# Selecting the top 128 keys of 32 attention heads: the row tiles of a head taken widest first instead of narrowest first

## The chip, the cores and the metric

The kernel runs on one core of a Trainium2 chip. A core has TensorE (PE, matmuls), VectorE (DVE), ScalarE (ACT), GpSimd (POOL) and SyncE (SP), each with an instruction stream of its own; they meet by semaphores. The metric is the time of one execution on the device in microseconds (us), lower is better. The kernel before takes 3154.21 us, the median of three runs (3152.70 to 3154.62).

## The reference, cut to what matters

The reference is a network of two layers on 1024 tokens: MLPs, a Mamba layer, and an attention layer with 32 heads of 16 features. The change is in the attention layer alone. There each row keeps its 128 largest causal scores and takes the softmax over these:

```python
draft = jnp.einsum('bhqd,bhkd->bhqk', qr, kr)
draft = draft + jnp.where(causal_future, neg, 0.0)
num_remain = max(min(Sq, MIN_REMAIN), Sq - int(Sq * MASK_OUT))      # 128 for Sq = 1024
_, draft_indices = jax.lax.top_k(draft, num_remain)
mask = jnp.full((B, H, Sq, Sq), neg).at[b_idx, h_idx, s_idx, draft_indices].set(0.0)
mask = jnp.where(causal_future, neg, mask)
scores = jnp.einsum('bhqd,bhkd->bhqk', qr, kr) / np.sqrt(HD) + mask
attn = jax.nn.softmax(scores, axis=-1)
out = jnp.einsum('bhqk,bhkd->bhqd', attn, v)
```

## The kernel before, in words

The function `attention_heads_fast` does the 32 heads. The 1024 query rows of a head are 8 row tiles of 128 rows; tile t needs only the keys up to its diagonal, (t + 1) * 128 columns. Tiles 1 to 7 (256 to 1024 columns) have more keys than 128 and need a selection; tile 0 has not. `W` is 7, `NT` is 8.

A head passes these steps. They lie in different iterations n of one loop, so that four or five heads are under way at once:

- *Scores and evacuation* (head n+1): PE computes the scores of a tile into `ps_z` (`scores`, L1943), DVE copies them to `z` in SBUF and keeps the row maximum (`evacuate`, L2256).
- *Sweeps* (heads n and n-1): ACT counts, per row, how many scores lie above a trial cut, by a Sign activation with an accumulator (`count`, L2090, the instruction is L2101). One sweep is seven counts, one for each tile. POOL then moves the trial cut (`move`, L2171). A head has four sweeps (k = 0 to 3); in an iteration ACT does (n, 0), (n-1, 2), (n, 1), (n-1, 3). The move behind sweep 3 gives the final cut (L2210), a little under 128 scores.
- *Marks and picks* (head n-2): DVE marks the scores above the cut (`take`, L2269), PE computes the scores again in `ps_m` with the marked ones put out of reach (`marked_scores`, L1959), DVE takes the eight largest that are left and replaces as many of them as are missing to 128 (`pick`, L2287: MAX8 at L2296, MATCH_REPLACE8 at L2304; `excess`, L2278, counts how many).
- *Exponents and values* (head n-3): for each chunk of up to four 128 column blocks of a tile PE turns the picked scores and subtracts the row maximum (`exponents`, L1997), ACT takes the exponential (`exponential`, L2105, the instruction is L2112), PE multiplies by V (`add_v`, L2022, done two chunks later). `CHUNKS` (L1820) numbers the 12 chunks of a head, in the order of the tiles.
- *Division* (head n-4) on DVE.

All orders are written out by hand. On PE the tables `CHUNK_AHEAD`, `CHUNKS_FIRST`, `CHUNKS_AFTER_MARKED` and `CHUNKS_AFTER_SCORES` say behind which tile's marked scores or scores a chunk's exponents stand. On ACT, `EXP_BEFORE` spreads the 12 Exps over the 28 counts of an iteration by the share of columns swept; each slot takes the Exp one chunk back (`LATER`). The buffers that tie the engines together: `ps_m` and `ps_z` have two banks each, which a tile of 640 columns or more fills, so the marked scores of the next wide tile wait for the pick of this one; `ps_e` has two buffers; marks and signs have two buffers. `stay_awake` issues seven filler matmuls a round into `ps_m`. The last heads have tables of their own (`LAST_BUT_ONE`, `LAST_CHUNKS`), and from head 29 on odd tiles put their marked scores in `ps_z`.

Of the kernel before, what the change touches and what calls it, by code (L numbers as in the profile page):

```python
# [1812 lines left out]
def attention_heads_fast(nc, env, X, qT, kT, v, mixed, q_tok, k_sums, ahead):  # L1813
# [27 lines left out]
    with ExitStack() as ctx:  # L1841
# [89 lines left out]
        def _(pe):  # L1931
# [27 lines left out]
            def marked_scores(h, t):  # L1959

                L, out = (t + 1) * P, marked_in(h, t)
                pe.wait_ge(take_done, h * W + t)
                if h < NO_SCORES:
                    done = h * W + t - 1 - (1 < t < 4)
                elif t >= 4:
                    done = h * W + t - 2
# [30 lines left out]
            def exponents(h, i):  # L1997
# [501 lines left out]
```

## Time and profile before

| | |
|---|---|
| median of 3 runs | 3154.21 us |
| profiled execution, its own time | 3158.36 us |
| its span, first to last instruction | 3156.5 us |
[...]
| PE, DVE, ACT, POOL busy over the span | 92%, 78%, 62%, 52% |
| stage of the heads | about 2067 to 3041 us |

The page of the profile covers the whole span, of which the heads are less than a third; the shares of the table are means over stages with different limits. The section of rows below therefore shows stretches of that stage. In a timeline a row is an instruction (or several merged, xN) with its start and duration; in brackets stands the idle time of the engine before it and what ended it. An ACT or DVE instruction's duration overlaps the next one's start by about 0.1 us, so distances between starts are what adds up.

### The profile page before, as it was taken

Reading aid. Unit: us, or ns where it says so; the run is one execution under the profiler, and the core shown is the slowest. Engines: PE = TensorE matmul, PEld = TensorE weight load, DVE = VectorE, ACT = ScalarE, POOL = GpSimd, SP = SyncE. Lnnn points to the kernel's source line nnn. Section 1 sums busy time; section 2 is a strip of 40 time slices with the busy share of each in tenths; the row PEclk is TensorE's granted clock in tenths of the full one; section 3 lists DMA queues with packets and bytes.
Section 4 is the critical chain, followed back from the end, with each engine's and each line's share of the span. In section 5 each row is a group of like instructions: output and inputs, shape, how many; then the busy total and the mean of one; then the engine's idle time right before and its main releaser. Section 6 shows DMA issues by size and latency. Waiting matters only on the chain. (4 is left out here: it accounts for less than half of the span.)

```text
span 3156.5 us, 50555 instructions
## 1 busy us (share of the span) xinstructions
PE 2899.5 (92%) x15929; PEld 1723.7 (55%) x15929; DVE 2461.0 (78%) x4633; ACT 1950.0 (62%) x4186; POOL 1651.6 (52%) x3659
## 2 busy tenths in 40 slices
PE   8899999999999999999999989847888888889889
PEld 4455455455454464454554554515666666667654
DVE  6678687697696796796876877749898899988846
ACT  2464554554564554554545533478999999999823
POOL 3236245254264263362462454767777777777613
PEclk9999999999999999999999999958899999998989
DMA  2223122232232132232221220000000000000000
GB/s 92 65 73 102 67 93 88 72 104 72 74 118 84 61 114 80 67 108 73 81 94 67 90 86 1 28 24 1 2 2 2 2 2 2 2 2 2 2 28 27
DMA packets 65947, 169.62 MB, mean 54 GB/s; under 512 B 11920, under 2 KB 19472, under 8 KB 64656
## 3 DMA queue, kind: packets, MB, share of 16 engines
q1 hardware_dynamic: 54016, 114.12, 11.5%
q10 hardware_dynamic: 11664, 52.24, 4.8%
q8 instruction: 131, 2.15, 0.3%
q14 instruction: 136, 1.11, 0.1%
HBM read 161.08 MB, written 5.24 MB: 53 GB/s over the span
## 5 line engine op out<-in xcount | busy, mean ns | idle before, releaser
L2101 ACT ACTIVATE X<-ah_z,ah_trial 128x256 bf16<-128x256 f32 (+6 forms) x896 | 736.3, 834 | 24.8 <-POOL ah_trial L2205 12.8
L1199 ACT ACTIVATE m_mix<-m_mix,m_cs 128x128 f32<-128x128 f32 x1024 | 312.9, 388 | 258.6 <-DMA m_mix<-cs_rows 258.6
L2031 PE MATMUL ah_ps_o<-a_v,X 128*128 128x17 f32 x2304 | 316.9, 264 | 0.1
L2031 PEld LDWEIGHTS ah_ps_o<-a_v,X 128*128 128x128 f32 x2304 | 300.0, 199 | 1.4 <-issue 0.2
L1081 POOL TENSOR_TENSOR m_xdec<-m_xdt,m_decay_out 128x512 f32<-128x512 f32 x112 | 141.4, 1262 | 213.0 <-DVE m_xdt L1325 202.1
L1109 POOL TENSOR_TENSOR m_squares<-m_squares 128x256 f32<-128x256 f32 x128 | 102.3, 799 | 277.5 <-ACT m_squares L1211 277.5
L2275 DVE TENSOR_SCALAR_CACHE_REDUCE X<-ah_z,ah_cut 128x256 bf16<-128x256 f32 (+6 forms) x224 | 193.8, 876 | 60.6 <-POOL ah_cut L2210 60.6
L1005 PE MATMUL m_ps_d<-m_w_out,m_gate 128*128 128x512 f32 x512 | 235.2, 602 | 0.0
L1005 PE MATMUL m_ps_x<-m_w_out,m_gate 128*128 128x512 f32 x512 | 233.7, 599 | 0.0
L2112 ACT ACTIVATE X<-ah_ps_e 128x512 f32<-128x512 f32 (+3 forms) x384 | 187.8, 490 | 62.7 <-PE ah_ps_e L2018 52.6
L2296 DVE MAX8 ah_top<-ah_ps_m 128x8 f32<-128x384 f32 (+6 forms) x215 | 177.1, 824 | 26.0 <-PE ah_ps_m L1983 25.3
L2266 DVE TENSOR_SCALAR_CACHE_REDUCE ah_z<-ah_ps_z 128x256 f32<-128x256 f32 (+6 forms) x224 | 182.5, 816 | 13.9 <-PE ah_ps_z L1955 13.9
L2197 POOL TENSOR_TENSOR ah_slope<-ah_between,ah_table 128x7 f32<-128x7 f32 x128 | 193.2, 1510 | 0.0
L1332 DVE TENSOR_TENSOR m_mix<-m_mix,m_cb 128x1024 f32<-128x1024 f32 x128 | 172.9, 1351 | 19.4 <-ACT m_mix L1202 19.0
L2101 ACT ACTIVATION_READ_ACCUMULATOR X<-ah_z,ah_trial 128x1 f32 x896 | 185.9, 207 | 0.0
L1979 PE MATMUL ah_ps_m<-a_kT,a_qT 128*128 128x512 bf16 (+3 forms) x337 | 107.0, 356 | 84.9 <-DVE tables L2304 84.9
L1172 ACT ACTIVATE m_xbc<-m_xbc 128x1024 f32<-128x1024 f32 x80 | 84.6, 1058 | 148.0 <-DVE m_xbc L1308 147.8
L2304 DVE MATCH_REPLACE8 tables<-ah_top,ah_ps_m 128x384 bf16<-128x384 f32 (+6 forms) x215 | 173.9, 809 | 0.3 <-issue 0.3
L1066 POOL TENSOR_TENSOR m_xdt<-m_w_proj 128x256 f32<-128x256 f32 x32 | 23.8, 742 | 286.1 <-PE m_ps_d L879 286.1
L1308 DVE SCALAR_TENSOR_TENSOR m_xbc<-m_b_tok,m_conv_p,m_xbc 128x1023 f32<-128x1023 f32 (+2 forms) x96 | 129.7, 1351 | 44.6 <-ACT m_xbc L1164 42.4
L879 PE MATMUL m_ps_y<-hT,m_w_proj 128*128 128x512 f32 x320 | 152.0, 597 | 5.3 <-ACT m_gate L1144 3.3
L973 PE MATMUL m_ps_c<-m_mix,m_xdt 128*64 128x128 f32 x2048 | 141.0, 280 | 16.6 <-DVE m_y L1351 8.4
(328 smaller groups left out, 7565.4 us busy)
## 6 DMA issues: line engine op xcount, KB each, us to landing
m_mix<-cs_rows SPq DMA_DIRECT2D x128, 512.0 KB, 4.4
m_w_proj<-in_w_proj ACTq DMA_DIRECT2D x69, 512.0 KB, 3.3
m_fade<-fade_rows SPq DMA_DIRECT2D x224, 128.0 KB, 3.0
m_w_out<-in_w_out ACTq DMA_DIRECT2D x7, 2048.0 KB, 7.8
X<-in_x SPq DMA_DIRECT2D x8, 256.0 KB, 6.4
m_w_out<-in_w_out SPq DMA_DIRECT2D x1, 2048.0 KB, 10.1
x_away<-X SPq DMA_DIRECT2D x1, 2048.0 KB, 7.3
out<-X SPq DMA_DIRECT2D x8, 256.0 KB, 2.0
```

Of the source, the lines that this page charges most:

```text
L879: last = pe.matmul(out, weights[:, k, :], tokens[:, k, :], start=start and k == 0, stop=stop and k == KH - 1, skip_group_check=True)
L1005: last = pe.matmul(ps_out[c % 2], gate[:, half * 4 + i, c * P:(c + 1) * P], w_out[:, half * 4 + i, :], start=(half == 0 and i == 0), stop= ...
L1199: act.activation(mix[:, u % 3, h, :], mix[:, u % 3, h, :], ACT.Relu, bias=cs[:, c, h0 + h:h0 + h + 1], scale=-1.0).then_inc(lag_done, 1)
L1332: dve.tensor_tensor(mix[:, u % 3], mix[:, u % 3], cb[:, c, :].unsqueeze(1).to_broadcast([P, HU, P]), ALU.mult).then_inc(mix_done, 1)
L2031: last = pe.matmul(ps_o[:, t, :], eT[:, g % 3, b * P:(b + 1) * P], v[:, b0 + b, h // REP, :], start=i == 0 and b == 0, stop=b0 + b == t, s ...
L2101: act.activation(sign[:, at % 2, 0:(t + 1) * P], z[:, h % RING, cols(t)], ACT.Sign, bias=trial[:, h % RING, 0, t - 1:t], scale=-1.0, accum ...
L2112: act.activation(eT[:, g % 3, 0:w * P], ps_e[g % 2][:, 0:w, :].rearrange("p b q -> p (b q)"), ACT.Exp, scale=0.25).then_inc(exp_done, 1)
L2197: pool.tensor_tensor(slope[:, 0], between[:, 1], table[:, 5], ALU.pow).then_inc(own, 1)
L2266: dve.tensor_scalar(z[:, h % RING, cols(t)], ps_z[:, z_at(t):z_at(t) + (t + 1) * P], 0.0, NEG, ALU.add, ALU.max, accum_out=row_max[:, h % ...
L2275: dve.tensor_scalar(mark[:, (h * W + t) % 2, 0:(t + 1) * P], z[:, h % RING, cols(t)], cut[:, h % 2, t - 1:t], 0.0, ALU.is_ge, ALU.add, acc ...
L2296: dve.max(top[:, r], marked_in(h, t)).then_inc(pick_step, 1)
L2304: dve.match_replace(picked[:, h % 2, cols(t)], top[:, r], marked_in(h, t), TAKEN).then_inc(pick_done, 1)
```

## The change

All engines take the tiles 7, 6, ..., 1 of a head instead of 1, 2, ..., 7: in scores and evacuation, sweeps, marks, marked scores and picks. The chunks are numbered from tile 7 down to tile 0, so the exponents, Exps and products with V follow that order too. The tables that place the chunks on PE are written anew, the slots for the Exps follow from the new order of column counts, and the semaphore values are computed by `place` and `z_place`. Tile 0's scores stay first. The rule for sharing `ps_m` and `ps_z` among the last three heads is adapted. No instruction is added or removed on PE, DVE and POOL; ACT's stream is the same but for merging of equal neighbours in listings.

```diff
+    ORDER = range(NT - 1, 0, -1)
-    CHUNKS = [(t, b) for t in range(NT) for b in range(0, t + 1, 4)]
+    CHUNKS = [(t, b) for t in range(NT - 1, -1, -1) for b in range(0, t + 1, 4)]
...
-    CHUNKS_AFTER_MARKED = ((), (), (), (), (), (7,), (9,), ())
-    CHUNKS_AFTER_SCORES = ((), (2,), (3, 4), (5,), (6,), (8,), (10,), (11,))
-    LAST_BUT_ONE = ((), (2, 3), (4, 5, 6), (7, 8, 9, 10, 11), (), (), (), ())
-    LAST_CHUNKS = ((), (), (), (), (0, 1), (2, 3), (4, 5), (6, 7))
+    CHUNKS_AFTER_MARKED = ((), (), (11,), (10,), (8,), (6,), (4,), (2,))
+    CHUNKS_AFTER_SCORES = ((), (), (), (), (9,), (7,), (5,), (3,))
...
+        place = lambda h, t: h * W + W - t
+        z_place = lambda h, t: h * NT + (NT - t) % NT
...
                 L, out = (t + 1) * P, marked_in(h, t)
-                pe.wait_ge(take_done, h * W + t)
+                at = place(h, t)
+                pe.wait_ge(take_done, at + 1)
                 if h < NO_SCORES:
-                    done = h * W + t - 1 - (1 < t < 4)
+                    done = at - (t < 3)
...
-                for t in range(1, NT):
+                for t in ORDER:
                     if live(n - 2):
                         marked_scores(n - 2, t)
                     if live(n - 3):
                         turn_and_add(n - 3, CHUNKS_AFTER_MARKED[t])
                     if live(n + 1):
                         scores(n + 1, t)
-                    if live(n - 2) and t == 4:
+                    if live(n - 2) and t == 5:
                         turned_rows(n - 2)
...
                 for back, k in sweeps_of(n):
-                    for t in range(1, NT):
+                    for t in ORDER:
...
                 if live(n - 2):
-                    take(n - 2, 1)
-                    take(n - 2, 2)
+                    take(n - 2, W)
+                    take(n - 2, W - 1)
                 if live(n - 4):
                     divide(n - 4)
-                for t in range(1, NT):
+                for t in ORDER:
                     if live(n - 2):
                         pick(n - 2, t)
                     if live(n + 1):
                         evacuate(n + 1, t)
-                    if live(n - 2) and t + 2 < NT:
-                        take(n - 2, t + 2)
+                    if live(n - 2) and t > 2:
+                        take(n - 2, t - 2)
```

In PE's instruction stream, behind the last filler matmuls of a round (the L2040 row, L2045 in the changed kernel, whose lines lie three to six further down), stand in the kernel before:

```order
L2040 MATMUL ah_ps_m<-a_kT,ident_bf 128x512 x3
L1977 MATMUL ah_ps_m<-future_bf,ident_bf 128x128
L1979 MATMUL ah_ps_m<-a_kT,a_qT 128x256
L1983 MATMUL ah_ps_m<-X,ah_ident_taken 128x256
L1953 MATMUL ah_ps_z<-future_bf,ident_bf 128x128
L1955 MATMUL ah_ps_z<-a_kT,a_qT 128x256
L2010 MATMUL ah_ps_e<-ah_ident_back,tables 128x128 x3
L2012 MATMUL ah_ps_e<-ah_rows,ah_minus_rows 128x384
L2015 MATMUL ah_ps_e<-a_qT,a_kT 128x128 x3
L2018 MATMUL ah_ps_e<-ident_bf,future_bf 128x128
```

and in the changed kernel:

```order
L2045 MATMUL ah_ps_m<-a_kT,ident_bf 128x512 x3
L1984 MATMUL ah_ps_m<-a_kT,a_qT 128x512
L1982 MATMUL ah_ps_m<-future_bf,ident_bf 128x128
L1984 MATMUL ah_ps_m<-a_kT,a_qT 128x512
L1988 MATMUL ah_ps_m<-X,ah_ident_taken 128x512 x2
L2015 MATMUL ah_ps_e<-ah_ident_back,tables 128x128 x4
L2017 MATMUL ah_ps_e<-ah_rows,ah_minus_rows 128x512
L2020 MATMUL ah_ps_e<-a_qT,a_kT 128x128 x4
L2036 MATMUL ah_ps_o<-a_v,X 128x17 x4
L1958 MATMUL ah_ps_z<-a_kT,a_qT 128x512
```

The first marked scores (`ah_ps_m`, L1977 to L1983) are those of the 1024 column tile instead of the 256 column one. The chunk of exponents (`ah_ps_e`) behind them has four blocks instead of three, and the new scores (`ah_ps_z`) stand behind this chunk.

In ACT's stream, from the first count of an iteration to the first of its second sweep, stand in the kernel before (L2101 is a count, L2112 an Exp):

```order
L2101 ACTIVATE X,ah_signs<-ah_z,ah_trial 128x256
L2112 ACTIVATE X<-ah_ps_e 128x512
L2101 ACTIVATE X,ah_signs<-ah_z,ah_trial 128x384
L2101 ACTIVATE X,ah_signs<-ah_z,ah_trial 128x512
L2101 ACTIVATE X,ah_signs<-ah_z,ah_trial 128x640
L2112 ACTIVATE X<-ah_ps_e 128x128
L2101 ACTIVATE X,ah_signs<-ah_z,ah_trial 128x768
L2112 ACTIVATE X<-ah_ps_e 128x256
L2101 ACTIVATE X,ah_signs<-ah_z,ah_trial 128x896
L2101 ACTIVATE X,ah_signs<-ah_z,ah_trial 128x1024
L2101 ACTIVATE X,ah_signs<-ah_z,ah_trial 128x256
L2112 ACTIVATE X<-ah_ps_e 128x384
```

and in the changed kernel, from the Exp that opens the iteration to the Exp that opens the second sweep:

```order
L2117 ACTIVATE X<-ah_ps_e 128x128
L2106 ACTIVATE X,ah_signs<-ah_z,ah_trial 128x1024
L2106 ACTIVATE X,ah_signs<-ah_z,ah_trial 128x896
L2117 ACTIVATE X<-ah_ps_e 128x512
L2106 ACTIVATE X,ah_signs<-ah_z,ah_trial 128x768
L2106 ACTIVATE X,ah_signs<-ah_z,ah_trial 128x640
L2117 ACTIVATE X<-ah_ps_e 128x512
L2106 ACTIVATE X,ah_signs<-ah_z,ah_trial 128x512
L2106 ACTIVATE X,ah_signs<-ah_z,ah_trial 128x384
L2106 ACTIVATE X,ah_signs<-ah_z,ah_trial 128x256
L2117 ACTIVATE X<-ah_ps_e 128x512
L2106 ACTIVATE X,ah_signs<-ah_z,ah_trial 128x1024
```

The counts fall from 1024 to 256 columns, the Exps of the first sweep are of 128, 512 and 512 columns, and the third chunk's Exp (chunk 2) stands ahead of the second sweep's first count instead of behind it.

In DVE's stream, from the first mark of a round (the L2275 row, L2281 in the changed kernel) to the first replacement, stand in the kernel before:

```order
L2275 TENSOR_SCALAR X,ah_taken_count<-ah_z,ah_cut 128x256
L2275 TENSOR_SCALAR X,ah_taken_count<-ah_z,ah_cut 128x384
L2311 RECIPROCAL ah_inv<-ah_ps_o 128x8
L2313 TENSOR_TENSOR hT<-ah_ps_o,ah_inv 128x8x16
L2284 TENSOR_SCALAR ah_surplus<-ah_ranks,ah_taken_count 128x8
L2296 MAX ah_top<-ah_ps_m 128x8
L2298 COPY_PREDICATED ah_top<-ah_surplus,ah_taken 128x8
L2284 TENSOR_SCALAR ah_surplus<-ah_ranks,ah_taken_count 128x8
L2304 MATCH_REPLACE tables<-ah_top,ah_ps_m 128x256
```

and in the changed kernel:

```order
L2281 TENSOR_SCALAR X,ah_taken_count<-ah_z,ah_cut 128x1024
L2281 TENSOR_SCALAR X,ah_taken_count<-ah_z,ah_cut 128x896
L2317 RECIPROCAL ah_inv<-ah_ps_o 128x8
L2319 TENSOR_TENSOR hT<-ah_ps_o,ah_inv 128x8x16
L2290 TENSOR_SCALAR ah_surplus<-ah_ranks,ah_taken_count 128x8
L2302 MAX ah_top<-ah_ps_m 128x8
L2304 COPY_PREDICATED ah_top<-ah_surplus,ah_taken 128x8
L2290 TENSOR_SCALAR ah_surplus<-ah_ranks,ah_taken_count 128x8
L2310 MATCH_REPLACE tables<-ah_top,ah_ps_m 128x1024
```

The two marks ahead of the first pick are the widest two, and the first pick is that of the widest tile.

## Rows read from the trace of the kernel before

**Rows 1.** Busy time by stretch; a round at half clock below:

```profile
core 0: us, PE busy (x) PEld busy (x) DVE busy (x) ACT busy (x) POOL busy (x), PEclk, DMA share, GB/s
2600.00:2700.00 100.00, 87.33 (x817) 67.46 (x816) 89.91 (x245) 97.53 (x247) 77.90 (x280) 0.97 0.01 2
2647.50:2654.00 6.50, 6.50 (x38) 4.93 (x36) 5.98 (x15) 4.67 (x13) 5.82 (x17) 0.51 0.00 1
```

**Rows 2.** Waits of ACT, 2200 to 2800 us: total, times, longest:

```profile
ACT X L2112 <- PE ah_ps_e L2018: 19.0, 22, 2.3
```

**Rows 3.** Timeline of DVE, first mark of a round: start, duration, names, idle before:

```profile
2181.87 0.48 DVE L2275 TENSOR_SCALAR_CACHE_REDUCE X<-ah_z,ah_cut 128x256 bf16<-128x256 f32 x1 [1.29 <-POOL ah_cut L2210]
...
2610.03 0.48 DVE L2275 TENSOR_SCALAR_CACHE_REDUCE X<-ah_z,ah_cut 128x256 bf16<-128x256 f32 x1 [1.10 <-POOL ah_cut L2210]
...
2637.83 0.48 DVE L2275 TENSOR_SCALAR_CACHE_REDUCE X<-ah_z,ah_cut 128x256 bf16<-128x256 f32 x1 [1.10 <-POOL ah_cut L2210]
...
2667.13 0.48 DVE L2275 TENSOR_SCALAR_CACHE_REDUCE X<-ah_z,ah_cut 128x256 bf16<-128x256 f32 x1 [1.87 <-POOL ah_cut L2210]
...
2951.32 0.48 DVE L2275 TENSOR_SCALAR_CACHE_REDUCE X<-ah_z,ah_cut 128x256 bf16<-128x256 f32 x1 [2.33 <-POOL ah_cut L2210]
```

**Rows 4.** Timeline of ACT, one iteration of 27.81 us:

```profile
2604.86 0.51 ACT L2101 ACTIVATE X<-ah_z,ah_trial 128x256 bf16<-128x256 f32 x1
...
2611.44 0.52 ACT L2101 ACTIVATE X<-ah_z,ah_trial 128x256 bf16<-128x256 f32 x1
...
2623.07 0.38 ACT L2112 ACTIVATE X<-ah_ps_e 128x256 f32<-128x256 f32 x1 [0.33 <-PE ah_ps_e L2018]
...
2632.67 0.51 ACT L2101 ACTIVATE X<-ah_z,ah_trial 128x256 bf16<-128x256 f32 x1
```

**Rows 5.** Timeline of POOL, first and last instructions of moves:

```profile
2618.65 0.21 POOL L2175 TENSOR_TENSOR ah_trial<-ah_signs,ah_table 128x7 f32<-128x7 f32 x1 [1.01 <-ACT X L2101]
...
2632.01 0.21 POOL L2205 TENSOR_TENSOR ah_trial<-ah_trial,ah_slope 128x7 f32<-128x7 f32 x1
2632.92 0.20 POOL L2175 TENSOR_TENSOR ah_trial<-ah_signs,ah_table 128x7 f32<-128x7 f32 x1 [0.70 <-ACT X L2101]
```

**Rows 6.** Timeline of PE, a 512 column matmul at half clock:

```profile
2647.51 0.63 PE L2012 MATMUL ah_ps_e<-ah_rows,ah_minus_rows 128*128 128x512 bf16 x1
```

**Rows 7.** Timeline of PE in an undisturbed round:

```profile
2610.58 0.23 PE L1977 MATMUL ah_ps_m<-future_bf,ident_bf 128*128 128x128 bf16 x1 [0.46 <-DVE X L2275]
...
2618.30 0.38 PE L1979 MATMUL ah_ps_m<-a_kT,a_qT 128*128 128x512 bf16 x1 [1.40 <-DVE tables L2304]
...
2622.81 0.22 PE L2018 MATMUL ah_ps_e<-ident_bf,future_bf 128*128 128x128 bf16 x1
...
2628.01 0.39 PE L2010 MATMUL ah_ps_e<-ah_ident_back,tables 128*128 128x128 bf16 x4
...
2628.67 1.02 PE L2031 MATMUL ah_ps_o<-a_v,X 128*128 128x17 f32 x8
2630.34 0.38 PE L1979 MATMUL ah_ps_m<-a_kT,a_qT 128*128 128x512 bf16 x1 [0.66 <-DVE tables L2304]
...
2631.26 0.39 PE L1955 MATMUL ah_ps_z<-a_kT,a_qT 128*128 128x512 bf16 x1
```

**Rows 8.** Timeline of DVE: a narrow mark's accumulator read, the widest mark:

```profile
2610.43 0.08 DVE L2275 DVE_READ_ACCUMULATOR X<-ah_z,ah_cut 128x1 f32 x1
...
2626.44 1.28 DVE L2275 TENSOR_SCALAR_CACHE_REDUCE X<-ah_z,ah_cut 128x1024 bf16<-128x1024 f32 x1
2627.64 0.08 DVE L2275 DVE_READ_ACCUMULATOR X<-ah_z,ah_cut 128x1 f32 x1
```

**Rows 9.** Instructions by line and shape, 2200 to 2800: busy, mean ns, idle before:

```profile
L2112 ACT ACTIVATE X<-ah_ps_e 128x512 f32<-128x512 f32 x127 | 75.7, 596 | 1.1 <-PE ah_ps_e L2015 1.1
...
L2296 DVE MAX8 ah_top<-ah_ps_m 128x8 f32<-128x1024 f32 x21 | 25.9, 1233 | 6.8 <-PE ah_ps_m L1983 6.8
...
L2304 DVE MATCH_REPLACE8 tables<-ah_top,ah_ps_m 128x1024 bf16<-128x1024 f32 x21 | 25.5, 1215 | 0.0
```

**Rows 10.** Timeline of PE, last products with V of the stage:

```profile
3037.69 3.08 PE L2031 MATMUL ah_ps_o<-a_v,X 128*128 128x17 f32 x22
```

More of the change, by code:

```diff
@@ L1836, in attention_heads_fast @@
     MOVE_AT = {hk: i for i, hk in enumerate(order)}
-    sign_share = np.cumsum([0] + [t + 1 for _ in SWEEPS for t in range(1, NT)])
+    sign_share = np.cumsum([0] + [t + 1 for _ in SWEEPS for t in ORDER])
     sign_share = sign_share / sign_share[-1]
@@ L1945, in scores @@
                 L, at = (t + 1) * P, z_at(t)
-                done = h * NT + t - (0 < t < 4)
-                if done:
+                done = z_place(h, t) - (t < 3)
+                if done > 0:
                     pe.wait_ge(z_done, done)
@@ L1982, in marked_scores @@
                     w = min(BANK, L - n)
-                    last = pe.matmul(out[:, n:n + w], ident_taken[:], mark[:, (h * W + t) % 2, n:n + w], start=False, stop=True,
+                    last = pe.matmul(out[:, n:n + w], ident_taken[:], mark[:, at % 2, n:n + w], start=False, stop=True,
                                      skip_group_check=True)
@@ L2006, in exponents @@
                 if t:
-                    pe.wait_ge(pick_done, h * W + t)
+                    pe.wait_ge(pick_done, place(h, t) + 1)
                     for b in range(w):
@@ L2269, in take @@
             def take(h, t):
-                if t == 1:
+                at = place(h, t)
+                if t == W:
                     dve.wait_ge(cut_done, h + 1)
-                if h * W + t > 2:
-                    dve.wait_ge(marked, h * W + t - 2)
-                dve.tensor_scalar(mark[:, (h * W + t) % 2, 0:(t + 1) * P], z[:, h % RING, cols(t)], cut[:, h % 2, t - 1:t], 0.0,
+                if at >= 2:
+                    dve.wait_ge(marked, at - 1)
+                dve.tensor_scalar(mark[:, at % 2, 0:(t + 1) * P], z[:, h % RING, cols(t)], cut[:, h % 2, t - 1:t], 0.0,
                                   ALU.is_ge, ALU.add, accum_out=taken_count[:, h, t - 1:t]).then_inc(take_done, 1)
             def excess(h, t):
-                at = h * W + t - 1
+                at = place(h, t)
                 if at >= 2:
@@ L2287, in pick @@
             def pick(h, t):
-                at = h * W + t - 1
+                at = place(h, t)
                 r = at % 2
@@ L2334, in _ @@
                 if live(n - 2):
-                    take(n - 2, 1)
-                    take(n - 2, 2)
+                    take(n - 2, W)
+                    take(n - 2, W - 1)
                 if live(n - 4):
                     divide(n - 4)
-                for t in range(1, NT):
+                for t in ORDER:
                     if live(n - 2):
@@ L2343, in _ @@
                         evacuate(n + 1, t)
-                    if live(n - 2) and t + 2 < NT:
-                        take(n - 2, t + 2)
+                    if live(n - 2) and t > 2:
+                        take(n - 2, t - 2)
             h = AH - 1
-            take(h, 1)
-            take(h, 2)
+            take(h, W)
+            take(h, W - 1)
             divide(h - 2)
-            for t in range(1, NT):
+            for t in ORDER:
                 pick(h, t)
-                if t + 2 < NT:
-                    take(h, t + 2)
-                if t == 4:
+                if t > 2:
+                    take(h, t - 2)
+                if t == 5:
                     divide(h - 1)
```

35 lines of the change are left out of this document (19 added, 16 removed).

## The prediction

> **What bounds the kernel now.** I first looked at where the change acts: the stage of the 32 heads, about 2067 to 3041 us. Outside it no instruction moves. The reader's first view is the busy time by stretch [rows 1]: of 100 us ScalarE (ACT) is busy 97.5, VectorE (DVE) 89.9, TensorE (PE) 87.3, GpSimd (POOL) 77.9. So ACT is nearly full, and what it still waits for matters: 19.0 us in 600, all of it for exponents (`ah_ps_e`) from PE [rows 2].
>
> Next I measured the round, which handles one head on every engine. It is the distance between two starts of the first mark on DVE, called T0 here. The 28 starts from 2181.87 to 2951.32 [rows 3] are 27 rounds in 769.45 us, 28.50 each. Of these, 12 last 27.80 to 27.82, as 2610.03 to 2637.83; 15 are longer, as the 29.30 to 2667.13. Against 27 x 27.80 = 750.6 the long ones cost 18.9 together.
>
> Then the timeline of one 27.80 us round tells what closes it. T0 is 2610.03; the Exp of 256 columns (chunk 7, tile 5, blocks 4 and 5) starts at 2623.07, after ACT waited 0.33 for it [rows 4]: 13.04 from T0. ACT's remaining work runs to 2632.67: 9.60. POOL starts the last move at 2632.92 [rows 5]: 0.25. The cut is out and the next T0 comes at 2637.83: 4.91. The sum is 27.80, the whole round. It is a loop, cut, marks and picks on DVE, exponents on PE, Exp and sweeps on ACT, move on POOL, back to the cut. ACT's own work is 2604.86 to 2632.67 less 0.33: 27.48. [...] The page's chain of waits shows nothing of this stage, so the argument goes by the timeline.
>
> **What the change moves.** No instruction is added or taken away, so the busy time of each engine stays. What moves is which chunk of exponents each Exp needs, when PE can have it, and where it stands among ACT's sweeps.
>
> *Chunk 2.* In the new order it is tile 6, blocks 0 to 3, placed on PE behind the marked scores of tile 7 (1024 columns); on ACT its Exp stands at the head of the second sweep. Today chunk 2 stands behind the marked scores of the 256 column tile. From T0 to its Exp, step by step:
> - the 1024 column mark on DVE, 2626.44 to 2627.64: 1.20 [rows 8];
> - from its accumulator read to PE, 2610.43 to 2610.58: 0.15 [rows 7, 8];
> - marked scores of tile 7 on PE, 2630.34 to 2631.26: 0.92 [rows 7];
> - exponents of four blocks, 2628.01 to 2628.67: 0.66 [rows 7];
> - from the last matmul to Exp, 2622.81 to 2623.07 less the matmul's own slot of 0.055 (a quarter of the 0.22 for four, from the same rows): 0.20 [rows 4, 7].
>
> That is 3.13 after T0. With 0.25 + 4.91 from the end of ACT's round to T0 it is 8.29 after ACT began its round. ACT wants it earlier. Its first sweep takes 2604.86 to 2611.44 = 6.58 today, with Exps of 512, 128 and 256 columns among the counts; in the new order they are 128, 512 and 512, so for one 0.60 stands instead of 0.38 [rows 4, 9]: about 6.79. ACT stands at that Exp for 8.29 - 6.79 = 1.50 us and, being in order, holds the sweep behind it. Behind it lie 27.48 - 6.79 = 20.69 of ACT's work. The new loop is 3.13 + 20.69 + 0.25 + 4.91 = 28.98, so 1.18 more than 27.80. Over 27 rounds: **+31.9 us**.
>
> *The other Exps.* The 0.33 that goes is in this sum already. The next tight place is chunk 4, behind the marked scores of tile 6, which wait for tile 7's pick. Two marks (1.20 and a little less), a maximum of 1.23 and a replacement of 1.22 [rows 9], and about 1.1 for the short operations between them put that pick's end near T0 + 5.8. PE adds a hand-over, marked scores and four blocks, near 1.9 in all: T0 + 7.7. ACT comes to that Exp at 3.13 and what stands between, two Exps and the counts of four wide tiles, near 7.8. That is an estimate by the rows above; it costs nothing, and at most 0.3 a round (two hand-overs of 0.15), +8 us.
>
> *POOL.* Between the second sweep's end and the last move it now works 2618.65 to 2632.21 = 13.56, and waits 0.70 [rows 5]. The third and fourth sweeps lose the 0.33 and have one Exp of 256 for one of 512 (-0.21). So 0.16 is left and POOL stays hidden, but only just.
>
> *DVE.* It waits 1.10 for the cut today [rows 3], and more in a longer round. The second mark (896 columns) covers PE's first marked scores, 0.92 [rows 7]. DVE's wait for PE at the last wide tiles goes; it lies behind the Exp that closes the loop, so I give it nothing. The evacuations that now come wide first are read by ACT a round later.
>
> *The clock of PE.* Today a half clock stretch costs a long round 18.9 / 15 = 1.26 on average, since the loop reaches PE only at chunk 7 with slack ahead. PE's long wait now is the 1.40 ahead of tile 4 [rows 7]. In the new order PE is done with its filler matmuls long before the 1024 column mark ends: today it waits 0.46 for a mark of 0.40 (2610.03 to 2610.43) [rows 3, 7, 8]; with the mark 0.80 and the round 1.18 longer that becomes about 2.4, and directly behind this wait stand the matmuls that the loop is made of. At half clock 0.92 + 0.66 = 1.58 is doubled at once, and the chunks behind it, which have 0.1 to 0.8 of slack, slip too. Bounds per fall: 1.58 and about 2.6 (half of the 6.5 us of such a stretch is 3.2, less the waits of 0.6 in it). I take 2.1, nearer the middle because both ends rest on rows, and 12 falls in 27 rounds, a little under today's 15 long ones, since some of those are only 0.3 to 0.5 long: 25 against 18.9, **+6**. With no falls it is -18.9; with one in each round +38.
>
> [...]
>
> *The ends of the stage.* At its start the evacuations pace ACT as before in sum: 0. At its end PE is the bound: its last 22 products run 3.08 from 3037.69 and end the stage [rows 10]. Ten chunks of head 30 and all of head 31 follow the last cut; in the new order chunks 0 and 1, done before it, hold 8 blocks, not 3. Five blocks of 0.66 / 4 and two products each of 0.11 to 0.14 (3.08 / 22) make 2.0 to 2.2, of which I take **-1.9 us**; the bounds are 0, if ACT's Exps pace the end, and -4.
>
> Sum: 31.9 + 6 - 1.9 = +36 on the profiled execution's 3158.4, which is 3194. That execution is 4.2 above the median of the runs, so the forecast is 3154.2 + 36 = 3190.
>
> **Rivals.**
> 1. *Few falls of the clock.* PE's waits are shared out otherwise and PE keeps full clock: 31.9 - 18.9 - 1.9 = +11, so 3165. For it: 12 of 27 rounds already run undisturbed. Against it: the longest wait grows.
> [...]
> 3. *Faster: ACT becomes the sole bound.* The place is the same Exp. If chunk 2 is ready by the 6.8 us at which ACT gets there, nothing holds ACT in any round, DVE's and PE's slack absorbs the clock, and a round is ACT's 27.48: 27 x (28.50 - 27.48) = 27.5 less, with the end 29 less, so 3125. It decides at a hand-over 1.5 us sooner than my sum. For it: most chunks get more time when the wide tiles are picked first. Against it: each of the five terms is a row.
> 4. *No difference*: about half the 1.50 is hidden by something that I take as serial, 27 x 0.5 less, and few falls: near 3154.
>
> **How the numbers follow.** Forecast (3176 to 3208) 0.55, rival 1 0.20, rival 2 0.12, rival 3 0.08, rival 4 0.05. About 0.2% is what a measurement of this kernel can tell from no change (6 us). The lower end of rival 1 gives 0.01 to "same": faster 0.08, same 0.06, slower 0.86. The range 3162 to 3220 holds the forecast, most of rival 1 and the lower part of rival 2, and leaves out rivals 3 and 4.
>
> **What would show it.** Right: a wait of ACT of about 1.5 us at the 512 column Exp that opens the second sweep, in each round, for PE; the 0.33 at the 256 column Exp gone; undisturbed rounds of 29.0; PE waiting about 2.4 for the 1024 column mark; POOL's wait before the last move near 0.16. Wrong: rounds of 27.5 and no such wait; or the wait at another Exp (chunk 4), or POOL without a wait ahead of the last move, which would make it the bound. If long rounds exceed 28.98 by under 1 us or are rare, the clock term is mis-sized and the time is nearer 3165.

## The result, and the profile after

The changed kernel takes 3246.9 us (median of 4 runs, 3232.56 to 3266.45) against 3153.9 for the kernel before: 1.0297 times as long, 95% interval 1.0271 to 1.0324. The forecast was 3190 with a range to 3220. The direction was right, the size was not. The profiled execution took 3232.56, the lowest of the four, with a span of 3230.7; before it was 3156.5 [rows 1 to 10 are from it]. The readings of this section compare these two spans, 74.2 apart. The medians are 93 apart: the profiled execution of before is 4 above its median, that of the changed kernel 14 below. The other three runs of the changed kernel have a lower mean clock (0.938 to 0.945 against 0.948; the profiled execution of before has 0.963), so more of the clock's loss is in them; no trace shows their rounds.

The busy time by stretch, columns as in [rows 1]: the same 100 us as there, then one undisturbed round, one long round, and the 27 us inside it.

```profile
2600.00:2700.00 100.00, 87.14 (x714) 67.39 (x714) 80.84 (x217) 86.45 (x218) 68.71 (x246) 0.85 0.01 2
...
2463.90:2492.78 28.88, 24.22 (x225) 18.84 (x226) 25.68 (x69) 27.12 (x69) 22.00 (x79) 0.94 0.01 2
2615.73:2653.31 37.58, 34.91 (x224) 27.46 (x225) 26.43 (x69) 27.70 (x68) 22.01 (x79) 0.64 0.00 1
2618.50:2645.50 27.00, 27.00 (x146) 21.32 (x145) 17.03 (x39) 18.69 (x44) 16.55 (x59) 0.50 0.00 1
```

ScalarE (ACT) fell from 97.53 to 86.45 busy in the same 100 us, and the granted clock from 0.97 to 0.85. The last line is the news: TensorE (PE) is busy 27.00 us out of 27.00, and its clock is 0.50 of full speed throughout. The two lines above it do the same work, one round: 69 or 68 instructions on ACT, about the same busy time on ACT, DVE and POOL. Only PE's busy time grew, from 24.22 to 34.91.

The first mark of a round on VectorE (DVE), now 1024 columns wide, is T0; it answers to [rows 3]:

```profile
2181.13 1.28 DVE L2281 TENSOR_SCALAR_CACHE_REDUCE X<-ah_z,ah_cut 128x1024 bf16<-128x1024 f32 x1 [2.31 <-POOL ah_cut L2215]
...
2463.90 1.28 DVE L2281 TENSOR_SCALAR_CACHE_REDUCE X<-ah_z,ah_cut 128x1024 bf16<-128x1024 f32 x1 [1.77 <-POOL ah_cut L2215]
...
2492.78 1.28 DVE L2281 TENSOR_SCALAR_CACHE_REDUCE X<-ah_z,ah_cut 128x1024 bf16<-128x1024 f32 x1 [0.63 <-POOL ah_cut L2215]
...
2615.73 1.28 DVE L2281 TENSOR_SCALAR_CACHE_REDUCE X<-ah_z,ah_cut 128x1024 bf16<-128x1024 f32 x1 [2.68 <-POOL ah_cut L2215]
...
2653.31 1.28 DVE L2281 TENSOR_SCALAR_CACHE_REDUCE X<-ah_z,ah_cut 128x1024 bf16<-128x1024 f32 x1
...
3026.67 1.28 DVE L2281 TENSOR_SCALAR_CACHE_REDUCE X<-ah_z,ah_cut 128x1024 bf16<-128x1024 f32 x1 [3.68 <-POOL ah_cut L2215]
```

From 2181.13 to 3026.67 there are 27 rounds in 845.54 us, 31.32 each. Nine of them take 28.88 to 28.91, as 2463.90 to 2492.78. The other 18 are longer, and three take 36 to 38. Split as the prediction was split:

| part | predicted | measured |
|---|---|---|
| undisturbed round, 27 of them against 27 x 27.80 | 28.98: +31.9 | 28.88: +29.2 |
| what the long rounds cost beyond that, less the 18.9 of before | 25 - 18.9 = +6 | 845.54 - 27 x 28.88 = 65.8, less 18.9 = +46.9 |
| before the first and behind the last of these T0 | -1.9 | (2181.13 - 2181.87) + (3230.7 - 3026.67) - (3156.5 - 2951.32) = -1.9 |
| sum of the spans | +36 | +74.2 |

Two of three terms stand; the term of the clock (25 - 18.9 in the second line) is wrong by 41 us. ACT's waits for exponents, 19.0 in the same 600 us before [rows 2], are now 71.0:

```profile
ACT X L2117 <- PE ah_ps_e L2020: 56.9, 28, 2.9
...
ACT X L2117 <- PE ah_ps_e L2023: 14.1, 18, 1.3
```

The undisturbed round from T0 = 2463.90, first ACT (as [rows 4]):

```profile
2467.04 0.60 ACT L2117 ACTIVATE X<-ah_ps_e 128x512 f32<-128x512 f32 x1 [1.40 <-PE ah_ps_e L2020]
...
2487.09 0.52 ACT L2106 ACTIVATE X<-ah_z,ah_trial 128x256 bf16<-128x256 f32 x1
...
2487.58 0.28 ACT L2117 ACTIVATE X<-ah_ps_e 128x128 f32<-128x128 f32 x1
```

then POOL (as [rows 5]):

```profile
2487.59 0.21 POOL L2210 TENSOR_TENSOR ah_trial<-ah_trial,ah_slope 128x7 f32<-128x7 f32 x1
2487.87 0.20 POOL L2180 TENSOR_TENSOR ah_trial<-ah_signs,ah_table 128x7 f32<-128x7 f32 x1
...
2492.54 0.20 POOL L2215 TENSOR_TENSOR ah_cut<-ah_trial,ah_slope 128x7 f32<-128x7 f32 x1
```

Chunk 2's Exp starts 3.14 after T0 (predicted 3.13) after a wait of 1.40 (1.50). ACT's work behind it ends at 2487.58: 20.54 (20.69). POOL's last move starts 0.29 later, and 4.91 after that comes the next T0: 28.88. It is the predicted loop. POOL has no wait left ahead of its last move (0.16 was predicted). It starts this move 0.29 behind ACT's last count where before it was 0.25, so POOL's three moves behind the second sweep now close the round by 0.04, with ACT's counts right beside them. Both paths begin at the wait for chunk 2, so the term is the same, but by these rows less work on ACT behind that sweep would no longer shorten the round.

PE in that round and in the long one (as [rows 6, 7]):

```profile
2465.24 0.39 PE L1984 MATMUL ah_ps_m<-a_kT,a_qT 128*128 128x512 bf16 x1 [2.27 <-DVE X L2281]
...
2617.07 0.39 PE L1984 MATMUL ah_ps_m<-a_kT,a_qT 128*128 128x512 bf16 x1 [3.17 <-DVE X L2281]
...
2618.22 0.46 PE L2017 MATMUL ah_ps_e<-ah_rows,ah_minus_rows 128*128 128x512 bf16 x1
...
2626.21 0.63 PE L2017 MATMUL ah_ps_e<-ah_rows,ah_minus_rows 128*128 128x512 bf16 x1
```

PE waits for the 1024 column mark 2.27 in one and 3.17 in the other (predicted 2.4). In the long round the first matmul behind the wait still takes 0.39. About 1.3 us after it began the clock falls, and it comes back only near 2646. From 2617 to 2646 ACT waits eight times for exponents, 9.3 us in all: each group of exponents is late at half clock.

### The profile page after: what moved, and what is told of

The parts are those of the page before. It is cut to its first block and busy times, and to the rows that moved or that the text cites. A ratio compares the mean times of both kernels' runs of the same rounds, so it can differ in the third digit from the quotient of the medians.

```text
span 3230.7 us, 50557 instructions
## 1 busy us (share of the span) xinstructions
PE 2944.9 (91%) x15929; PEld 1757.8 (54%) x15929; DVE 2462.4 (76%) x4633; ACT 1954.7 (61%) x4186; POOL 1650.7 (51%) x3659
## 5 line engine op out<-in xcount | busy, mean ns | idle before, releaser
L2106 ACT ACTIVATE X<-ah_z,ah_trial 128x1024 bf16<-128x1024 f32 (+6 forms) x896 | 734.8, 832 | 19.1 <-POOL ah_trial L2168 9.9
L2036 PE MATMUL ah_ps_o<-a_v,X 128*128 128x17 f32 x2304 | 337.5, 274 | 0.0
L2036 PEld LDWEIGHTS ah_ps_o<-a_v,X 128*128 128x128 f32 x2304 | 322.5, 212 | 0.0
L2281 DVE TENSOR_SCALAR_CACHE_REDUCE X<-ah_z,ah_cut 128x1024 bf16<-128x1024 f32 (+6 forms) x224 | 193.6, 875 | 85.1 <-POOL ah_cut L2215 85.0
L2271 DVE TENSOR_SCALAR_CACHE_REDUCE ah_z<-ah_ps_z 128x1024 f32<-128x1024 f32 (+6 forms) x224 | 182.7, 817 | 32.4 <-PE ah_ps_z L1958 32.0
L2302 DVE MAX8 ah_top<-ah_ps_m 128x8 f32<-128x640 f32 (+6 forms) x215 | 176.8, 822 | 39.1 <-PE ah_ps_m L1988 37.7
L2310 DVE MATCH_REPLACE8 tables<-ah_top,ah_ps_m 128x640 bf16<-128x640 f32 (+6 forms) x215 | 173.9, 809 | 0.3 <-issue 0.3
```

The costliest lines, as they stand in the source:

```text
L2036: last = pe.matmul(ps_o[:, t, :], eT[:, g % 3, b * P:(b + 1) * P], v[:, b0 + b, h // REP, :], start=i == 0 and b == 0, stop=b0 + b == t, s ...
L2106: act.activation(sign[:, at % 2, 0:(t + 1) * P], z[:, h % RING, cols(t)], ACT.Sign, bias=trial[:, h % RING, 0, t - 1:t], scale=-1.0, accum ...
L2271: dve.tensor_scalar(z[:, h % RING, cols(t)], ps_z[:, z_at(t):z_at(t) + (t + 1) * P], 0.0, NEG, ALU.add, ALU.max, accum_out=row_max[:, h % ...
L2281: dve.tensor_scalar(mark[:, at % 2, 0:(t + 1) * P], z[:, h % RING, cols(t)], cut[:, h % 2, t - 1:t], 0.0, ALU.is_ge, ALU.add, accum_out=ta ...
L2302: dve.max(top[:, r], marked_in(h, t)).then_inc(pick_step, 1)
L2310: dve.match_replace(picked[:, h % 2, cols(t)], top[:, r], marked_in(h, t), TAKEN).then_inc(pick_done, 1)
```

## Experiments

What I wanted to tell apart: theory A, that the base is the loop through chunk 2 and the rest are falls of the clock that start at PE's wait for the 1024 column mark and then hold on; against it, that the long rounds come from other waits and the clock only follows.  "Round" is the undisturbed one; the clock is the mean granted clock from 2210 to 2950 us of the profiled execution.

| run | time, us | ratio to before, 95% | round | clock |
|---|---|---|---|---|
| before | 3153 to 3157 | 1 | 27.80 | 0.94 |
| changed | 3246.9 | 1.0271 to 1.0324 | 28.88 | 0.89 |
| e2: changed, no fillers | 3273.3 | 1.0357 to 1.0440 | 28.91 (one) | 0.81 |
| g3: changed, 11 fillers a round | 3169.1 | 1.0039 to 1.0078 | 28.88 | 0.99 |
| e1: changed, 16 fillers a round | 3171.5 | 1.0035 to 1.0069 | 28.88 | 0.99 |
| e4: changed, divisions first | 3232.8 | 1.0235 to 1.0295 | 28.88 | 0.91 |
| e3: e4 and chunk 2 ahead | 3149.9 | 0.9982 to 1.0013 | 28.12 | 0.99 |
| f1: changed, Exps later | 3188.7 | 1.0087 to 1.0146 | 28.23 | 0.97 |
| f3: e3 and chunk 4 ahead | 3167.9 | 1.0019 to 1.0048 | 27.89 | 0.94 |
| f4: f3, Exps later | 3155.8 | 0.9986 to 1.0010 | 27.89 | 0.95 |
| g1: e3, Exps later | 3145.6 | 0.9961 to 0.9979 | 27.87 | 0.98 |
| g2: e1, Exps later | 3189.8 | 1.0101 to 1.0132 | 28.3 | 0.99 |
| f2: before, no fillers | 3175.4 | 1.0044 to 1.0077 | 28.46 | 0.90 |
| g4: before, Exps later | 3127.5 | 0.9894 to 0.9924 | 27.38 | 0.98 |

### More fillers, fewer, none (e1_fill, g3_fill7, e2_nofill)

```diff
 e1:                    stay_awake(n - 2, 3)  ->  stay_awake(n - 2, 12)
 g3:                    stay_awake(n - 2, 3)  ->  stay_awake(n - 2, 7)
 e2: both calls of stay_awake in the loop of rounds taken out
```

> The changed kernel with 12 instead of 3 filler matmuls behind chunk 1 in each round, so that TensorE works through most of the 2.4 us in which it otherwise waits for the 1024 column mark. Nothing else moves; at full clock nine fillers are 9 x 0.21 = 1.9 us, which fit into the wait. Theory A (the base of the loss is the loop through chunk 2, 28.9 us a round; the rest is half clock that starts at this wait and then holds itself up, since at half clock TensorE paces the loop): the half clock falls from 178 us of the stage to under 100, the undisturbed round stays 28.9, the excess of the long rounds falls from 66 us to 10 to 35, time 3190 to 3217. Rival B (the long rounds have another cause, the clock only follows them): half clock and time as they are, 3240 or more. Rival C (the fillers run late at half clock and push the marked scores back): slower than the changed kernel, 3255 or more.

> The changed kernel without the seven filler matmuls of a round. Theory A (falls of the clock start at TensorE's waits at the head of a round): more or longer falls, half clock above 178 us of the stage, time 3265 to 3400, by up to about 2.5 us in each of 30 rounds that is not yet long. Rival B (the clock only follows): within 0.2% of the changed kernel, 3240 to 3253. Rival C (fillers themselves stand in the way of the marked scores in slow rounds): faster, under 3240.

> The changed kernel with 7 instead of 3 fillers behind chunk 1: four fillers or 0.85 us cover a third of TensorE's wait for the 1024 column mark, which stays at about 1.6 us. With 0, 7 and 16 fillers a round the times were 3273, 3247 and 3171.5. Theory A in its plain form (falls in proportion to the wait left): 3247 - 75 x 4/9 = 3213 (3200 to 3225). Rival B (a step: the falls go only when the wait is nearly covered): 3235 to 3250. Rival C (a step in the other direction: 1.6 us of wait is short enough): 3170 to 3185.

The lines of waits for PE at the marked scores, 2210 to 2950 us (total, times, longest), in the changed kernel:

```profile
PE ah_ps_m L1984 <- DVE X L2281: 62.6, 24, 3.4
```

in e2:

```profile
PE ah_ps_m L1984 <- DVE X L2277: 112.9, 22, 5.3
```

in g3:

```profile
PE ah_ps_m L1984 <- DVE X L2281: 32.7, 21, 1.9
```

and in e1:

```profile
PE ah_ps_m L1984 <- DVE X L2281: 11.1, 21, 0.9
```

The wait is 5.1 on average without fillers, 2.6 with 7, 1.6 with 11, 0.5 with 16. The time goes 3273, 3247, 3169, 3172. That is not in proportion to the wait; three quarters of the gain come between 7 and 11 fillers, where rival C of g3 had put the time. In e2 the matmul right behind the wait is already slow, and PE then stays slow while fully busy:

```profile
2373.17 0.61 PE L1984 MATMUL ah_ps_m<-a_kT,a_qT 128*128 128x512 bf16 x1 [5.17 <-DVE X L2277]
```

```profile
2373.50:2392.50 19.00, 19.00 (x98) 14.41 (x96) 12.63 (x28) 10.65 (x25) 10.21 (x39) 0.50 0.00 1
```

In g3 the matmul behind the wait of 1.86 runs at full clock, and the rounds have no spread left: 26 of them fill the 751.25 us between these two marks, 28.89 each, none over 29.06.

```profile
2411.76 0.39 PE L1984 MATMUL ah_ps_m<-a_kT,a_qT 128*128 128x512 bf16 x1 [1.86 <-DVE X L2281]
```

```profile
2208.07 1.28 DVE L2281 TENSOR_SCALAR_CACHE_REDUCE X<-ah_z,ah_cut 128x1024 bf16<-128x1024 f32 x1 [2.00 <-POOL ah_cut L2215]
...
2959.32 1.28 DVE L2281 TENSOR_SCALAR_CACHE_REDUCE X<-ah_z,ah_cut 128x1024 bf16<-128x1024 f32 x1 [3.74 <-POOL ah_cut L2215]
```

ACT still waits for chunk 2 in g3 (35.3 in 740 us for L2020, 26 times). So g3 is the changed order's own loop nearly without falls (clock 0.99), and it is 13 us above before in the same comparison. Of the 93 us by the medians 78 go with 4 fillers, which add nothing but work for PE. This takes away the long rounds that the kernel before had too (18.9 us), so the clock costs the changed kernel about 60 more than it cost before. e1 came out at 3171.5, below its expected 3190 to 3217: I had left it 10 to 35 us of long rounds where 4 are left, and had taken the excess from the profiled execution but the time from the median, 14 higher. e2 lengthened nearly every round, to 30.4, 33.8 or 36.2.

### Chunk 2 ahead of the mark, and its control (e3_chunk_ahead, e4_divide_only)

```diff
-    CHUNKS_FIRST = (1,)
+    CHUNKS_FIRST = (1, 2)
-    CHUNKS_AFTER_MARKED = ((), (), (11,), (10,), (8,), (6,), (4,), (2,))
+    CHUNKS_AFTER_MARKED = ((), (), (11,), (10,), (8,), (6,), (4,), ())
 DVE (e3 and e4): divide(n - 4) ahead of take(n - 2, W), take(n - 2, W - 1)
```

> The changed kernel with chunk 2 (four blocks of tile 6, head n-3) placed on TensorE ahead of tile 7's marked scores instead of behind them, and on VectorE the divisions of head n-4 ahead of the two first marks instead of behind them (so the sums of V that chunk 2 brings with it find their bank free). Theory A (the loop of 28.9 us is closed by chunk 2's Exp behind the mark and marked scores of tile 7): that wait of ScalarE goes, undisturbed rounds come to 27.5 to 27.9, TensorE has 1.6 us less of its long wait; time 3247 - 27 x 1.2 = 3215 if the long rounds keep their excess, 3140 to 3185 if it shrinks with the wait. Rival B (another wait, POOL's moves or the picks, closes the round at 28.9): rounds of 28.9, time 3235 or more.

> Control for the run before: the changed kernel with only the divisions on VectorE moved ahead of the first two marks, chunk 2 left where it is. Theory A: the divisions fall into VectorE's wait for the cut and nothing of the loop through chunk 2 moves: undisturbed rounds 28.9, time 3235 to 3255. Rival B (VectorE's order at the head of the round is what counts): rounds shorter by the 0.4 to 0.7 of the divisions, 3215 to 3235.

e3 takes away 97 us, all that the change had cost, and can't be told from the kernel before (0.9982 to 1.0013); e4 takes away 14 and keeps the round of 28.88, just under its expected 3235. The 14 are not clear of the spread (the intervals in the table overlap); they lie in the range of e4's rival B, but its shorter rounds did not come. It is chunk 2's place that counts. The move does two things at once: it takes chunk 2 out of the loop (28.88 to 28.12), and it fills PE's wait with real work: the waits ahead of the first marked scores come to 6.9 us in 740, 0.4 each, and the clock to 0.99. A round of e3, from T0 to T0 on DVE, and ACT's only wait in it:

```profile
2322.21 1.28 DVE L2281 TENSOR_SCALAR_CACHE_REDUCE X<-ah_z,ah_cut 128x1024 bf16<-128x1024 f32 x1 [0.88 <-POOL ah_cut L2215]
...
2350.33 1.28 DVE L2281 TENSOR_SCALAR_CACHE_REDUCE X<-ah_z,ah_cut 128x1024 bf16<-128x1024 f32 x1 [0.87 <-POOL ah_cut L2215]
```

```profile
2329.33 0.60 ACT L2117 ACTIVATE X<-ah_ps_e 128x512 f32<-128x512 f32 x1 [0.64 <-PE ah_ps_e L2020]
```

The wait stands 7.1 after T0, at chunk 4's Exp, which the prediction had named as the next tight place. POOL again has no wait ahead of its last move.

### The Exps later among ScalarE's counts (f1_exps_later, g2_fill_later)

```diff
-    EXP_BEFORE = [[i for i in range(NCH) if lo <= (i + 0.3) / NCH < hi] ...]
+    EXP_BEFORE = [[i for i in range(NCH) if lo <= (i + 0.7) / NCH < hi] ...]
```

> The changed kernel with the Exps of a round placed later among ScalarE's counts (a share of 0.7 instead of 0.3): chunk 2's Exp stands behind the 1024 column count of the second sweep instead of ahead of it, 1.1 to 1.3 us later; TensorE's order is untouched, and so is its 2.5 us wait for the 1024 column mark. Theory A (the base of the loss is ScalarE's wait at that Exp; the falls come from TensorE's wait, and chunk 2 behind it sets what they cost): the wait of 1.4 falls to 0.2 to 0.4, undisturbed rounds 27.8 to 28.1, time 3247 - 27 x 0.9 = 3222 with the falls as they are, 3185 to 3222 with slack added to them. Rival B (the picks or the moves bound the round at 28.9): rounds of 28.9, 3240 or more.

> The changed kernel with both cures that leave TensorE's order of chunks alone: 12 instead of 3 fillers (e1) and the later Exps (f1). Theory A (two terms that add: the falls behind the wait, and ScalarE's wait at chunk 2's Exp): the loop is 28.9 - 1.1 = 27.8, or the 28.2 of f1 where chunk 3 and half clock fillers close it; time 3171.5 - 27 x 0.9 = 3147 (3142 to 3158), the level of the kernel before. Rival B (not additive: the fillers push chunk 2 back as far as the Exps were moved): 3160 or more.

In f1 the wait at chunk 2's Exp fell to 0.21, and chunk 3's now has 0.31 behind it:

```profile
2362.67 0.60 ACT L2117 ACTIVATE X<-ah_ps_e 128x512 f32<-128x512 f32 x1 [0.21 <-PE ah_ps_e L2020]
2364.60 0.49 ACT L2117 ACTIVATE X<-ah_ps_e 128x384 f32<-128x384 f32 x1 [0.31 <-PE ah_ps_e L2023]
```

The round is 28.23, 0.65 less; the time is 58 less than the changed kernel's, so more than 27 x 0.65 = 18 came back: the clock rose to 0.97. The expectation had PE's wait for the 1024 column mark untouched; it fell too, to 46.3 us in 24 waits, 1.9 each. The runs spread from 3170 to 3201, and the profiled one is the lowest, with three rounds of 32.4 to 32.6. g2 was a miss. Both cures together give 3189.8, where 3147 was expected and e1 alone has 3171.5. Its profiled execution took 3162.78, the other four 3188.7 to 3194.3, so the trace doesn't show the 27 us in question. In it the cures do add in part: rounds of 28.3, and 9 us under e1's profiled execution. The other four have a mean clock of 0.964 to 0.965 against its 0.974, so their loss goes with the clock. What lowers it there, and so whether rival B's reason holds, stays open; by the medians the two cures don't add.

### Two chunks ahead (f3_two_ahead, f4_two_ahead_later)

```diff
 f3, from e3:
-    CHUNKS_AFTER_MARKED = ((), (), (11,), (10,), (8,), (6,), (4,), ())
-    CHUNKS_AFTER_SCORES = ((), (), (), (), (9,), (7,), (5,), (3,))
+    CHUNKS_AFTER_MARKED = ((), (), (11,), (10,), (8,), (6,), (), ())
+    CHUNKS_AFTER_SCORES = ((), (), (), (), (9,), (7,), (5,), (3, 4))
 f4: f3 with (i + 0.7) / NCH
```

> As e3_chunk_ahead, and chunk 4 (tile 5, blocks 0 to 3) right behind chunk 3 on TensorE, ahead of tile 6's marked scores instead of behind them. In e3 the undisturbed round was 28.12 with one wait of ScalarE in it, 0.66 at chunk 4's Exp. Theory A (that wait closes the round): it goes, rounds of 27.46 to 27.6, half clock not more than in e3 (22 us of the stage), time 3150 - 27 x 0.6 = 3134 (3128 to 3140). Rival B (a loop of 28.1 lies elsewhere, by the moves or the picks): rounds of 28.1, 3146 to 3153. Rival C (exponents in front delay tile 6's marked scores and so the picks): over 3155.

> As f3_two_ahead, with the Exps later among the counts as in f1_exps_later. Theory A (in f3 ScalarE waits for nothing in an undisturbed round, its 27.5 of work is the bound): no more to be had from later Exps, 3128 to 3142, and less spread by falls. Rival B (the exponents' two banks come free later and TensorE waits for them): 3140 to 3160.

f3 shortened the undisturbed round to 27.89, not 27.5, and the kernel got 18 us slower than e3. Chunk 4 had been what PE did between two marked scores. With it gone to the front PE waits there in one piece:

```profile
2314.27 0.22 PE L1982 MATMUL ah_ps_m<-future_bf,ident_bf 128*128 128x128 bf16 x1 [2.09 <-DVE tables L2310]
```

and the clock is back at 0.94; 12 of 26 rounds take over 29.9. The clock falls behind that wait:

```profile
2342.17:2343.00 0.83, 0.83 (x9) 0.67 (x9) 0.83 (x3) 0.83 (x2) 0.67 (x5) 1.00 0.00 0
2343.50:2349.50 6.00, 6.00 (x36) 4.81 (x34) 4.73 (x12) 4.39 (x12) 5.23 (x16) 0.50 0.00 0
```

The 2.09 is too long by about 0.2: the record of the first matmul behind the wait is missing in this trace, and its weight load stands at 2314.03. The time is in the range of rival C (over 3155), but the undisturbed round got shorter, so its reason, later picks, isn't what happened. None of the three expectations had a fall of the clock; it is the prediction's error a second time. f4 has the same round of 27.89 and loses less to the clock (long rounds of 29.2 instead of 30.2).

### The kernel before under the same edits (f2_before_nofill, g4_before_later)

```diff
 f2: both calls of stay_awake in the loop of rounds taken out
 g4, from before:
-    EXP_BEFORE = [[i for i in range(NCH) if lo <= (i + 0.3) / NCH < hi] ...]
+    EXP_BEFORE = [[i for i in range(NCH) if lo <= (i + 0.6) / NCH < hi] ...]
```

> The kernel before without its seven filler matmuls of a round: what the same loss of TensorE's work costs where the loop reaches TensorE only at chunk 7. In the changed kernel it cost 26 us and took half clock from 178 to 290 us of the stage. Theory A (falls cost much only where exponents stand behind a wait of TensorE with no slack): half clock rises from 85 us of the stage, but less than in the changed kernel, and the time rises by 0 to 20, 3155 to 3175. Rival B (fillers matter alike in both orders): 3175 to 3190. Rival C (the fillers did nothing here): 3152 to 3157.

> The kernel before with its Exps later among the counts (a share of 0.6 instead of 0.3; chunk 7's Exp about one count later, with the others of its place). Its undisturbed round of 27.80 was read as closed by chunk 7's Exp, with ScalarE waiting 0.33 there and 27.48 of work. Theory A: the wait goes, undisturbed rounds 27.48 to 27.55, time 3154 - 27 x 0.3 = 3146 (3140 to 3150). Rival B (the round of before was closed by something else): rounds of 27.8, 3152 to 3157. Rival C (the exponents' banks come free later and TensorE waits more, the clock falls more): over 3160.

f2 cost 18 us against before in the same comparison, at the border between its expectations A and B; the changed kernel lost 26 by the same edit. It doesn't show that the old order bears a loss of fillers much better, as I had thought.

g4 was a miss on the fast side (3140 to 3150 was expected). It is the fastest kernel here: 3127.5, 0.9% under the kernel before. Its waits of ACT for exponents in 740 us are

```profile
ACT X L2112 <- PE ah_ps_e L2018: 3.2, 4, 1.2
```

where before had 25.0 in 27 waits, and its busy time by stretch shows ACT at 736.10 of 740:

```profile
2210.00:2950.00 740.00, 629.01 (x5972) 497.61 (x6081) 685.55 (x1844) 736.10 (x1853) 592.72 (x2122) 0.98 0.01 2
```

The round is 27.38, the 27.80 less chunk 7's wait of 0.33 and 0.09 more. Of the 29 us, 27 x 0.42 = 11 are the loop; the rest is excess of long rounds that no longer reaches the end, since 24 of 26 rounds from 2210.68 take 27.30 to 27.44. The clock rose from 0.94 to 0.98, though PE's longest wait for a pick is 1.7 where it was 1.8; why the falls went isn't shown.

### The wide order, mended (g1_ahead_later)

```diff
 e3 with (i + 0.7) / NCH
```

> e3_chunk_ahead (chunk 2 ahead of tile 7's marked scores, divisions first) with the Exps later among the counts as in f1_exps_later. In e3 the undisturbed round was 28.12 with ScalarE waiting 0.66 at chunk 4's Exp; that Exp now comes one 384 column count (0.5) later. Theory A (that wait closes e3's round, and the falls stay as rare as in e3, since TensorE's order and waits stay): rounds of 27.6 to 27.8, half clock about as in e3, time 3150 - 27 x 0.4 = 3139 (3130 to 3146), below the kernel before. Rival B (a tighter round makes TensorE's waits fall otherwise and the clock takes it back, as in f3 and f4): 3146 to 3165.

3145.6, 0.2% to 0.4% under the kernel before and 18 over g4. The round is 27.87, at the edge of what was expected, with 0.34 of the 0.64 left at chunk 4's Exp.

## Why the prediction was right in its mechanism and wrong in its size

- **The loop** through the 1024 column mark, tile 7's marked scores, chunk 2 and its Exp was right: 28.88 for 28.98, and each part within 0.15. g3 shows it alone, e3 takes it away.
- **The other Exps and POOL**: chunk 4 cost nothing while chunk 2 held the round, and became the limit at 28.12 once it was gone, as its small slack had said. POOL's slack was 0.00 for 0.16. The prediction had called POOL without this wait a sign of being wrong, since it would be the bound. The sign came, and by 0.04 POOL is the bound behind the second sweep; the round stayed at 28.88 only because POOL's path hangs on the same wait for chunk 2.
- **The ends of the stage**: -1.9 for -1.9.
- **PE's wait** ahead of the marked scores was right too: 2.27 in the undisturbed round and 2.6 on average for about 2.4.
- **The clock, the step that failed.** The prediction said: "I take 2.1 [...] and 12 falls in 27 rounds [...] **+6**", and 38 for a fall in every round. It took a fall at this wait to double the matmuls of one stretch of about 6.5 us, and so bounded a fall by 2.6. The stretch is that of [rows 1], with the clock at 0.51 over 2647.5 to 2654 against 0.97 over the 100 us, where a 512 column matmul takes 0.63 [rows 6] against 0.38 [rows 7]. That it doubles the loop's own matmuls (1.58) was an estimate, and e2 nearly shows it: from the first marked scores to the end of four blocks of exponents it is 1.61 at full clock (2465.24 to 2466.85 in the changed kernel) and 3.07 at half (2373.17 to 2376.24 in e2). Measured are 18 long rounds at 65.8 / 18 = 3.7 each, up to 8.8. Of the 41 us, 6 x 2.1 = 13 are the number of falls and 18 x 1.6 = 28 the price of each. A stretch at half clock is not of given length. In [rows 1] it was over after 6.5 us; here it ran 27.0. With the clock at 0.64 over the long round PE has 34.9 us of work in 37.6 and everybody waits for it, where with 0.94 it has 24.2 in 28.9: the fall makes PE the bound of the round, and it stays at half clock although it is never idle. My upper bound rested on the length of one stretch, which is not a bound; the same trace of before has one of 9 us and more, which the prediction didn't look at:

```profile
2275.50:2284.50 9.00, 8.62 (x47) 6.42 (x48) 7.69 (x19) 6.05 (x18) 7.73 (x27) 0.50 0.00 1
```

The traces give the share of the half clock that reached the end. The clock is 1.00 or 0.50 in the stretches shown, and over the 740 us its mean is 0.89 in the changed kernel and 0.94 before. From these means I estimate 2 x (1 - 0.89) x 740 = 163 us at half clock in the changed kernel and 89 before. The long rounds in the same stretch cost 61 (725.64 for 23 rounds of 28.88) and 18 (741.2 for 26 of 27.80): before, a fifth of the time at half clock reached the end, now three eighths. A fall in each turn of the loop is what e2 shows, 22 falls at 22 waits of 5.1 to 5.3; the changed kernel had 18 long rounds in 27.

Rival 1 (few falls, 3165) had the mechanism of the base right; g3 is this rival, made by four matmuls, at 3169. Rival 2, a fall in each round for the wait of 2.4, was nearest in time (31.9 + 38 - 1.9 = 68, so 3222) and right in naming that wait. That such a wait brings a fall in every round was not shown by the trace of before, where full clock follows a wait of 1.40 (0.38 for the matmul [rows 7]), and the changed kernel does not show it either. And it priced a fall at the same 2.1, (38 + 18.9) / 27; the falls were fewer and dearer, 18 at 3.7. That the wait is the cause is supported by e3, which fills it without adding work, and by f3, where a wait of about 1.9 elsewhere brought the clock down again. The places of the falls say the same. Between 2210 and 2950 us the changed kernel's clock falls 18 times, 17 of them during the wait for the 1024 column mark or within 1.4 us of its end. In f3 it falls 14 times, 11 of them within 1.1 us of the end of the new wait. In g3, e1 and e3 it falls 4, 4 and 6 times, never there but each time 24 to 26 us after T0, and for 3 to 4 us. What is not explained is why one turn of the loop brings a fall and the next does not. The length of the wait doesn't tell: in the changed kernel full clock goes on at first behind one of 3.44 and half clock is there behind one of 2.58, and in f3 waits of equal length come with and without a fall.

```profile
2398.69 0.39 PE L1984 MATMUL ah_ps_m<-a_kT,a_qT 128*128 128x512 bf16 x1 [3.44 <-DVE X L2281]
...
2683.56 0.61 PE L1984 MATMUL ah_ps_m<-a_kT,a_qT 128*128 128x512 bf16 x1 [2.58 <-DVE X L2281]
```

And g2 stays open.

## What to carry to other kernels

Where a stage runs one engine close to full load, read for each reordering where it gathers TensorE's idle time into one piece ahead of the matmuls of the loop: here one wait of 2.6 a round cost the clock (0.89), and the same work in e3, with no wait above 1.7, did not (0.99). These lengths are no threshold: the kernel before, with waits up to 1.8, had 0.94. Price a fall by asking whether TensorE's work at half clock would still fit in the round (34.9, with the clock at 0.64, did not fit in 28.9), not by the length of the stretches seen so far. And try the cheap shift of a consumer first: moving the Exps one count later took out the wait that the profile of before had shown all along (0.33 a round) and was worth more than any of the orders, 11 us by that wait and 17 by the rarer long rounds.

## What the runs showed of the hardware that I had not expected

- TensorE stayed at 0.50 of its clock for 27.0 us in which it was busy for all 27.00 by the profile, and for 19.0 in e2. Steady work by that measure did not bring the clock back sooner.
- Four matmuls of 512 columns a round, 0.85 us of work (g3's seven fillers take 1.67) whose result nobody reads, took 78 us off 3247, and nine gave no more (3169 and 3172).
- A fall can stand in the wait or behind it. After each of e2's 22 waits of 5.1 to 5.3 the first matmul is at half clock (0.61). In the changed kernel it is so after some waits (2.58), while after others (3.17, 3.44) the first is at full clock (0.39) and the clock falls about 1.3 us later.
